# A decoder block's causal self attention: queries and keys in two 4-byte parts instead of three 2-byte ones, even and odd heads in the two halves of the array's rows, loops written out

## What is computed

```python
x = x + _L0_attn_ref(_layernorm(x, axis=-1), ...)     # self attention, changed
x = x + _L0_xattn_ref(_layernorm(x, axis=-1), ctx_1024, ctx_1024, mask, ...)
x = x + _L0_ffn_ref(_layernorm(x, axis=-1), ...)

# self attention; both score terms are folded into one set of key-side weights
Q = (x @ Wq.T + bq).reshape(b, s, H, hd)              # H = 16, hd = 16, s = 1024
K = (x @ Wk.T + bk).reshape(b, s, H, hd)
V = (x @ Wv.T + bv).reshape(b, s, H, hd)
scores = (gt * scores_cross + (1.0 - gt) * scores_conv) * scale
scores = jnp.where(causal[None, None], scores, -jnp.inf)
attn = jax.nn.softmax(scores, axis=-1)
out = jnp.einsum('bhqk,bkhd->bqhd', attn, V).reshape(b, s, H * hd)
```

## Time and profile before

| | |
|---|---|
| median of 3 runs (lowest, highest) | 1246.96 us (1246.66, 1250.59) |
| span of the profiled execution | 1246.4 us |
| the profiled execution's own time | no more than its span is on record; 0.6 us lie between it and the median |
| PE, VectorE, ScalarE, GpSimd busy | 1081.7, 792.2, 557.3, 216.0 us |
| DMA | 153.3 MB, 123 GB/s on average |
| block 2 | about 47 to 149 us |
| block 3 (self attention), with its first maxima | 134.6 to 682 us |
| block 4, cross attention | 687 to 815, 815 to 980 us |
| feed-forward | 999 to 1246 us |

### The profile page before, as it was taken

How to read it: one execution, slowest core, us unless ns; L and a number is a source line. 1 busy time by engine, 2 the same in 40 slices (tenths; PEclk the granted TensorE clock), 3 DMA queues, 4 the chain that set the end, 5 groups by cost and what they waited for, 6 DMA issues and landing times. The chain is left out here.

```text
span 1246.4 us, 23540 instructions
## 1 busy us (share of the span) xinstructions
PE 1081.7 (87%) x7116; PEld 640.1 (51%) x7164; DVE 792.2 (64%) x1705; ACT 557.3 (45%) x1022; POOL 216.0 (17%) x175
## 2 busy tenths in 40 slices
PE   1888969998999899999998665769999689999997
PEld 1677424443444344444443443434444278888886
DVE  4799837776777777777781775745555255555452
ACT  2456126665666666666666111216666321111110
POOL 4155510000000000000001233310000133333321
PEclk9899769998999989999999777859999889999999
DMA  6389892443344434444022578885666422222200
GB/s 196 104 289 309 252 149 70 85 91 71 75 86 87 87 69 86 86 87 90 18 74 87 170 218 234 245 235 148 173 177 163 148 68 68 68 67 67 67 18 34
DMA packets 132838, 153.30 MB, mean 123 GB/s; under 512 B 29003, under 2 KB 104319, under 8 KB 132735
## 3 DMA queue, kind: packets, MB, share of 16 engines
q1 hardware_dynamic: 126207, 145.74, 45.5%
q10 hardware_dynamic: 6528, 6.29, 1.5%
HBM read 87.69 MB, written 64.95 MB: 122 GB/s over the span
## 5 line engine op out<-in xcount | busy, mean ns | idle before, releaser
L687 DVE TENSOR_REDUCE self_pm<-bank 128x1 f32<-128x512 f32 (+3 forms) x608 | 365.4, 656 | 100.0 <-PE bank L772 68.7
L738 ACT ACTIVATE self_prob<-bank 128x512 f32<-128x512 f32 (+1 forms) x608 | 325.6, 577 | 184.1 <-PE bank L794 110.1
L786 PE MATMUL bank<-self_stq,self_stk 98*128 98x512 bf16 (+3 forms) x768 | 225.7, 334 | 24.9 <-DMA self_stq<-self_mrow 11.8
L763 PE MATMUL bank<-self_stk,self_stq 96*128 96x512 bf16 (+3 forms) x768 | 228.7, 342 | 8.1 <-DVE self_mrow L684 5.4
L806 PE MATMUL bank<-self_prob,self_va 128*32 128x512 f32 (+3 forms) x1536 | 163.7, 507 | 4.3
L763 PEld LDWEIGHTS bank<-self_stk,self_stq 96*128 96x128 bf16 x768 | 71.2, 100 | 162.4 <-DVE self_pm L687 111.8
L961 POOL TENSOR_TENSOR rin<-rin,bo_b 128x1024 f32<-128x1024 f32 x8 | 26.1, 3259 | 538.1 <-DMA min_<-mask_BxSxS_bk 538.1
L1768 ACT ACTIVATE e_sg<-bank 128x512 f32<-128x512 f32 x48 | 28.7, 599 | 191.9 <-PE bank L184 191.9
L786 PEld LDWEIGHTS bank<-self_stq,self_stk 98*128 98x128 bf16 x768 | 70.1, 99 | 83.8 <-issue 32.0
L738 ACT ACTIVATE cross_prob<-bank 96x512 f32<-96x512 f32 x128 | 74.8, 593 | 63.2 <-PE bank L791 63.0
L687 DVE TENSOR_REDUCE cross_pm<-bank 128x4 f32<-128x384 f32 x128 | 70.0, 557 | 35.0 <-PE bank L768 33.2
(11 more groups left out here) (189 smaller groups left out, 1423.9 us busy)
## 6 DMA issues: line engine op xcount, KB each, us to landing
qk<-a_parts SPq DMA_DIRECT2D x32, 384.0 KB, 4.8
self_stq<-qk SPq DMA_DIRECT2D x192, 64.0 KB, 2.9
self_stk<-qk SPq DMA_DIRECT2D x96, 128.0 KB, 5.2
cross_stq<-xqs SPq DMA_DIRECT2D x32, 384.0 KB, 4.7
vs<-a_vst SPq DMA_DIRECT2D x8, 1024.0 KB, 5.5
self_va<-vs SPq DMA_DIRECT2D x16, 512.0 KB, 7.0
od<-self_u SPq DMA_DIRECT2D x16, 512.0 KB, 2.7
oin<-od SPq DMA_DIRECT2D x32, 256.0 KB
```

Of the source, the lines that this page charges most:

```text
L687: nc.vector.tensor_reduce(pm[:, k, h0:h0 + hb, r], src[:, 0:hb * w].rearrange("p (h w) -> p h w", h=hb), AX, ALU.max).then_inc(s_mxe, 1)
L738: nc.scalar.activation(ops.prob[:, u % NPS, 0:hb * n], bank[ST_BANKS[u % 3]][0:KP, 0:hb * n], ACT.Exp).then_inc(s_ex, 1)
L763: mm = nc.tensor.matmul(dst[:, h * w:(h + 1) * w], stq[i][0:R, half, h0 + h, r * P:(r + 1) * P], stk[i][0:R, h0 + h, k0:k0 + w], start=(h ...
L786: mm = nc.tensor.matmul(dst[0:KP, h * n:(h + 1) * n], stk[i][0:RM, h0 + h, kt * KP:(kt + 1) * KP], stq[i][0:RM, half, h0 + h, q0:q0 + n], ...
```

## The change

`self_attention` is a new function for block 3 alone; `attention` stays for cross attention.

- Queries and keys are cut in two parts of 4 bytes (the F32R type, which the feed-forward already uses), and three products of parts are formed: 48 rows per head instead of 96, 50 with the maxima.
- Even heads lie on partitions 0 to 49, odd heads on 64 to 113, and each product is made of pairs, one in each half of the array's rows, into two different banks. Each kind still has three banks. A pair waits for both.
- The triangles are made in products of 64 rows too, two per bank, of 64 columns per head, with a bf16 stationary matrix `pick` and a moving one `off` which GpSimd builds in block 1 by a chain of some forty small steps.
- The values have 17 columns per head instead of 32; the maxima are kept as two 4-byte parts, turned in float32, and sent by four DMAs of 2 rows instead of two of 1 row.
- In block 2 the third part falls away, and so do the second pass of ScalarE and the pass of GpSimd; a chunk is written by eight DMAs of 256 KB instead of four of 384 KB. A group is loaded by nine DMAs instead of 19.
- The rows of -1 are set by fills of 32 partitions from partition 32 and 96 on, which overlap rows that the loads fill; so SP waits for the fills before it loads. Three of the four groups' fills are made after the barrier that ends block 2.
- All loops of all blocks are written out.

```diff
+Q_CUTS = ((0, 0, 1), (1, 0, 2))
+K_CUTS = ((0, 0, 2), (2, 0, 1))
+SELF_BANKS = (0, 1, 2), (3, 4, 5), (6, 7)
-    qk3 = dram("qk3", (2, 3, G, HG * HD, S), BF16)
-    vs = dram("vs", (G, P, S // P, HG * VW), F32)
+    qk2 = dram("qk2", (2, B * H, 2, HD, S), F32)
+    vs = dram("vs", (G, P, S // P, (HD + 1) * HG), F32)
-            with eng.Fori(0, B - peeled) as b:
-                chunk(b, 0, True)
-                chunk(b, 1, True)
-            for b in range(B - peeled, B):
+        def sweep(chunk):
+            for b in range(B):
                 chunk(b, 0, True)
                 chunk(b, 1, b < B - 1)
...
+        def self_attention(stage, ops, o_dst, following):
+            NPS = 12
+            MXB, STB, PVB = SELF_BANKS
...
+            LAG = 2
+            LATE = 2
...
+            for p in range(NSP):
+                plan.append(("s", p, 0))
+                if p == LATE:
+                    plan.append(("r", (NMX - 1,), 0))
+                upto = max(0, p - LATE + 1) * len(items) // (NSP - LATE)
+                plan += [("r", n, 1) for n in items[at:upto]]
+                at = upto
+                plan += [("p", s, 0) for s, x in enumerate(sets) if x[3] - 1 == p - LAG]
...
+                def maxima(g, c):
+                    sp.wait_ge(s_mxe, NMB + g * NMX + ring.index(("t", c)) + 1)
+                    for par in range(2):
+                        for hh in range(2):
+                            at = 16 * par + 8 * hh
+                            sp.dma_start(stq[g % GB][64 * par + ML:64 * par + SL, hh, c * 512:(c + 1) * 512].bitcast(F32),
+                                         mrow[at:at + 8, g % 2, c].bitcast(F32)).then_inc(md[g % 2][c], 16)
...
+                            nc.gpsimd.memset(stk[i][64 * par + 32:64 * par + 64].bitcast(F32), -1.0).then_inc(s_set, 1)
...
+                def maxima(g, ns):
+                    t.wait_ge(s_mxe, g * NMX + ns[-1] + 1)
...
+                    for j in range(len(hs[0])):
+                        for par in range(2):
+                            rows = slice(64 * par, 64 * par + ML)
+                            mm = nc.tensor.matmul(dst[par][:, j * w:(j + 1) * w],
+                                                  stq[i][rows, hs[par][j], (4 * half + r) * P:(4 * half + r + 1) * P],
+                                                  stk[i][rows, hs[par][j], k0:k0 + w],
+                                                  start=(j == 0), stop=not diag, skip_group_check=True)
...
+                    for c in range(2):
+                        for par in range(2):
+                            rows = slice(64 * par, 64 * par + 64)
+                            k1 = w - P + c * P // 2
+                            mm = nc.tensor.matmul(
+                                dst[par][:, 0:len(hs[0]) * w].rearrange("p (h w) -> p h w", w=w)[:, :, k1:k1 + P // 2],
+                                pick[rows, 0, c], off[rows, 0, 0:len(hs[0])], start=False, stop=(c == 1), skip_group_check=True)
...
+                def scores(g, p):
+                    if p == 0 or p == half_end[0]:
+                        t.wait_ge(md[g % 2][half], 64 * (g // 2 + 1))
+                    t.wait_ge(s_ex, U + 2)
...
+                barrier(g, 2)
+                self_gpsimd(g, False)
...
+                self_placed(sp, GB)
                 load_group(sp, self_ops, 0, 1)
                 self_sync(sp, True)
                 load_group(sp, self_ops, 0, 2)
```

More of the change, by code:

```diff
@@ L372, in _, with step, where @@
                 power1(g, 0, 0)
+                halfp = P // 2
+                made = [0]
+                def step(ins):
+                    ins.then_inc(s_pk, 1)
+                    made[0] += 1
+                    g.wait_ge(s_pk, made[0])
+                def where(ap, op, fill, base, pattern, slope):
+                    step(nc.gpsimd.affine_select(out=ap, in_=ap, compare_op=op, fill=fill, base=base,
+                                                 pattern=pattern, channel_multiplier=slope))
@@ L373, in _ @@
+                nc.gpsimd.tensor_copy(pick[:], pickf[:])
+                for i in range(2):
+                    nc.gpsimd.tensor_copy(off[:, :, i], offf[:, :, 0])
                 power1(g, 0, 1)
@@ L618, in attention, with steps @@
             stq, stk, va, mk, ld, NLD = ops.stq, ops.stk, ops.va, ops.mk, ops.ld, ops.n_loads
-            def steps(eng, step):
-                with eng.Fori(0, B - 1) as b:
-                    for i in range(GB):
-                        step(b, i, GB)
-                for i in range(GB):
-                    step(B - 1, i, GB - 1 - i)
+            def steps(step):
+                for g in range(G):
+                    step(g // GB, g % GB, min(GB, G - 1 - g))
             def after(b, i, n):
@@ L874, in place, with __init__ @@
                         self.mk.append(sb(f"{self.name}mk{i}", [SK, S], BF16))
+        class SelfOperands:
+            def __init__(self, load_qk, n_qk, v_src):
+                self.stq, self.stk, self.va = [], [], []
+                self.load_qk, self.v_src, self.m_src = load_qk, v_src, None
+                self.ld = [sem(f"self_ld{i}") for i in range(GB)]
+                self.n_loads = n_qk + 1
+            def place(self, n):
+                for i in range(len(self.stq), len(self.stq) + n):
+                    self.stq.append(sb(f"self_stq{i}", [P, HG // 2, S], F32R))
+                    self.stk.append(sb(f"self_stk{i}", [P, HG // 2, S], F32R))
+                    self.va.append(sb(f"self_va{i}", [P, S // P, HD + 1, HG]))
         def load_group(sp, ops, b, i):
@@ L1014, in program @@
             xnt = sb("a_xnt", [P, 2, 2, KT, CH], F32R)
-            parts = sb("a_parts", [P, 2, 4, 3, CH], BF16)
-            rest = sb("a_rest", [P, 4, CH])
-            vst = sb("a_vst", [P, 2, GB, J, HG, VW])
+            parts = sb("a_parts", [P, 2, 4, 2, CH], F32R)
+            vst = sb("a_vst", [P, 2, GB, J, HD + 1, HG])
             s_xh = sem("a_xh")
```

421 lines of the change are left out of this document (330 added, 91 removed).

## The result

The changed kernel takes **1397.03 us** (median of 3 runs, 1382.8 to 1398.76) against 1246.96 before: 1.116 times as long, 95% interval 1.108 to 1.124. 1190 was forecast, range 1155 to 1238. The profiled execution has a span of 1397.0 us, 150.6 more than before.

The account below looks back on a forecast made before the run. PE's list was taken to bound self attention, its group falling from 31.0 to 28.0 us. The terms - 45 - 2 - 14 - 4 + 8 = - 57 on a span of 1246.4 gave 1190 us, range 1155 to 1238.

Parts of the forecast that it names:

- Pairing: Self attention: the two products of a pair, one in each half of the array's rows, run together.
- rival (c): Self attention: the halves of the rows do not run together, 33.8 to 36.5 us per group, 1300 in all; chance 0.11.
- PE's list, 27.1 us: Self attention: PE's products, switches, seam and residue per group, the middle between 24.6 and 29.5 us.
- the lower end: Self attention: both halves load and multiply side by side, a pair costing one product; PE's list 24.6 us per group.
- VectorE 24.4, ScalarE 21.6: Self attention: busy us of these two engines per group after the change, both below PE's middle sum.
- Coupling. A pair waits for two banks of three ...: Self attention: pairs wait for banks and the group's maxima may land late; 0.9 us per group added for both.
- I am wrong if ... the granted clock falls in self attention: Self attention: a sign against the forecast, the clock falling because PE is less busy; no size given.
- Loops, - 14: Self attention: two loop ends cost 7.0 us each, which writing the loops out removes.
- Block 2, - 4: Block 2: normalisation on VectorE is shorter without GpSimd's pass, 4 us less over 7 chunks; bytes stay about 3 MB.
- Start of block 3, + 8: After the barrier, fills, loads and DMAs delay the first scores to 24.5 us instead of 16.9; cost 8.
- Rival (b): Self attention: pairs work, but loads come one after the other and late maxima stall; 30.5 us per group, 1235; chance 0.17.

Follow-up runs that it names:

- e3: The changed kernel with four banks for the maxima instead of three and one for the values instead of two: 1280.57 us, ratio 1.025.
- e11: The kernel before, loops written out, self attention's maxima and scores products issued two by two, the first waiting for both banks: 1280.85 us, ratio 1.026.
- e12: The kernel before, loops written out, self attention's maxima and scores products issued two by two, each waiting for its own bank alone: 1245.73 us, ratio 0.998.
- e1: The kernel before with all loops written out and nothing else: 1234.07 us, ratio 0.989.
- e2: The changed kernel with stores of 128 rows by 512 columns, same number and bytes, a group loaded by 13 DMAs instead of 9: 1362.19 us.
- e10: The kernel before, loops written out, with four banks for the maxima and one for the values in self attention alone: 1232.69 us, ratio 0.988.
- e7: The changed kernel with stores of 128 rows by 512 columns, four banks for the maxima and one for the values: 1243.86 us, ratio 0.996.
- e9: The changed kernel with 128-row stores and four maxima banks, and SP sending group 0's maxima before it waits for the fills: 1242.39 us, ratio 0.995.
- e13: The kernel before, loops written out, products two by two; first of two maxima products waits for all three banks, of two scores for both: 1358.29 us.

## Why the prediction was wrong, point by point

- **Pairing, rival (c)**: right that they run together. 0.24 to 0.34 for a pair of 512 columns.
- **PE's list, 27.1 us**: near, in part by luck. e3's group has PE busy for 27.21, but busy time holds no waits and the 27.1 held 2.1 of them; a triangle's four products took 0.07 where the lower end had 0.11, and a pair 0.24 to 0.34 where it had 0.234. The rule that the Trainium skill states in TensorEngine Tiling (Array Packing), Key Properties, that different tiles load and multiply in parallel, is borne out for the two halves of the rows as far as 0.24 for a pair goes; the 24.6 us that it would give are not reached, and VectorE never became the bound.
- **VectorE 24.4, ScalarE 21.6**: near, 24.5 to 25.0 and 20.8.
- **"Coupling. A pair waits for two banks of three ..."**: this is the step that failed. The mechanism was named and sized at 0.9 us with the maxima's DMAs. The late maxima that filled most of it hardly occur (2.7 us in all behind the start). The best group takes 3.75 us more than e3's (34.25 - 30.50): 1.7 of them are PE busy for longer (28.93 against 27.21) at a clock of 0.95, and 2.0 are the wait for two banks of three, as much as e11 shows against e12 (2.1). With a fourth bank PE still stands 3.3 in a group (30.50 - 27.21), 2.7 of them for ScalarE's exponentials, where the sum had 2.1 of small waits. I had worked out one step of four maxima and taken the engines as if each could work ahead. My reading, which the runs bear out in size only: with two of three banks claimed at once, VectorE or ScalarE empties one bank while PE stands, and PE fills two while they stand. The pair at 388.71 waited 0.78 for VectorE, the ones at 386.97 and 391.40 0.45 and 0.37 for ScalarE. e11 against e12 shows the wait by itself, where a product is one and not a pair's half.
- **"I am wrong if ... the granted clock falls in self attention"**: it did. This is the second step that failed, and the larger: the fall was named as a sign, but had no term in the sum and no rival. From 215.19 to 758.50, from one group's turned maxima to those 14 groups later, a group takes 38.8 on average, 4.6 more than the best one; all but the two best are at 0.53 to 0.89 of the clock. With the 1.7 in the best group that is 6.3 a group, some 94 us in 15. The wait proper is 15 x 2.0 = 30, and e3's group is 0.5 shorter than before's 31.0. Nearly all of both vanishes with the fourth bank: e3 is 116.5 faster. That the wait brings the fall in this kernel is shown by e3; why it falls so far is open. The kernel before held a hint that I passed over: a loop's end with 3.3 us of standing cost 3.9 more by the clock.
- **Loops, - 14**: right (e1: - 14.2).
- **Block 2, - 4, "Bytes in and out of a chunk stay about 3 MB"**: failed, + 37. The bytes did stay (6.3 MB in two chunks); what changed is the shape of the stores, with which the DMA engines' share fell from 0.88 to 0.65 and SP's queue, held up, ran full. I costed bytes and neither shape nor issue time. e2, with as many stores, gives it all back and ends block 2 7 us earlier than before, where 4 was forecast.
- **Start of block 3, + 8**: right (+ 8.3).
- **Rival (b)**: its sum comes to 1236 and not 1235 (1246.4 + 0.6 - 11); nothing hangs on it.

In sum the terms give: 37 stores, 8 start, - 14 loops, and 120 for self attention's groups (105.6 + 14), where 30 + 94 - 8 = 116 are found. Rival (c), 1300, had the right side for a wrong reason.

What would beat both kernels is the kernel before with its loops written out (e1, 1234.07; with the fourth bank, e10, 1232.69). The changed self attention with both repairs (e7, 1243.86; e9, 1242.39) comes to before's time and not under e1: its group of 30.4 us is hardly shorter than before's 31.0.

## What to carry to other kernels

A product of two parts that needs two buffers of a ring halves the ring: count how many such steps the ring holds (three banks: one and a half), not how many banks, and give the ring whose consumer is slowest a bank before asking what the products cost. Look at the shapes of DMAs beside their bytes, above all when one queue issues all of them. The timeline shows whether that queue is full; compare the issue time of one and the same DMA in a quiet place and in the crowd before blaming the issue itself. Price the clock too when a change adds waits to PE: here it cost three times what the waits did. Take from a change what stands alone (here the loops) and measure it alone.

## What the runs showed of the hardware

- Stores of 8 x 16 partitions x 512 columns of 4 bytes took SP 1.24 us each to issue (median), stores of 128 x 512, as many bytes, 0.50. In windows of two chunks the DMA engines moved 217 GB/s at a share of 0.65 with the first and 338 at 1.00 with the second. The issue of a load among the first kind rose from 0.54 to 2.17.
- TensorE's granted clock switches between its two levels, 1.2 and 2.4 GHz, inside a steady run of like groups. In windows of 50 us it was 0.51 to 1.00 with the same products. In the changed kernel and e3 it went with PE's waits: 1.00 in e3 with PE busy 27.21 of 30.50 us, 0.95 in the changed kernel's best group with 28.93 of 34.25. Across kernels it did not: e13 kept 1.00 with 31.54 of 38.52. After a fall the products last longer, so PE looks busier (45.35 of 48.90): a high busy share at a low clock is no sign of a well-fed engine.
- Pairs of 4-byte products in the two halves of the rows, 512 columns each: 0.24 us to the next start where the pair followed another such pair (409.58 to 409.82), 0.34 where it followed a set of values (390.14 to 390.48).
